# Attention probabilities left unnormalised, split in SBUF and transposed by DMA, with the outputs scaled in PSUM

## What is computed

```python
scores = jnp.einsum('bhqd,bhkd->bhqk', q, k) / scale
scores = jnp.where(causal[None, None], scores, -jnp.inf)
attn = jax.nn.softmax(scores, axis=-1)
out = jnp.einsum('bhqk,bhkd->bhqd', attn, v)
out = out.transpose(0, 2, 1, 3).reshape(B, S, N_HEADS * HEAD_DIM)
return out @ Wo
```

## Time and profile before

| | us |
|---|---|
| median of 3 runs | 739.17 (738.39 to 739.94) |
| the profiled execution | 737.62 |
| span of its instructions | 735.7 |
| attention loop rounds (from round 4 on), each | 31.52 |
| rounds 0 to 3 | 37.31, 39.92, 39.91, 34.10 |
| last round and epilogue | 35.1 |
| from there to the end | 163.5 |

### The profile page before, as it was taken

One profiled execution on the slowest core, in us unless ns is written; L12 is line 12 of the kernel. 1 busy time (PEld: TensorE's weight loads), 2 busy tenths in 40 slices (PEclk: granted clock), 3 DMA queues, 4 the chain that ended last, 5 costly groups with the idle time before them and its releaser, 6 DMA issues.

```text
span 735.7 us, 17233 instructions
## 1 busy us (share of the span) xinstructions
PE 659.1 (90%) x4994; PEld 460.8 (63%) x4995; DVE 581.6 (79%) x1683; ACT 442.3 (60%) x1205; POOL 537.8 (73%) x588
## 2 busy tenths in 40 slices
PE   3678869789999999999999999999987899999992
PEld 1255546556766667676666766667665577767761
DVE  6988879789999999998999999999876344333378
ACT  3585636465657666575675657668584664555542
POOL 4677777978888887888877888888988993555510
PEclk9899989999999999999999999999998999999996
DMA  9491000500000000000000000000122564665772
GB/s 306 165 301 48 1 0 2 141 22 16 0 14 14 0 14 0 14 7 7 14 0 14 0 14 14 0 14 2 35 70 88 167 117 105 138 141 138 210 285 101
DMA packets 64952, 50.44 MB, mean 69 GB/s; under 512 B 35252, under 2 KB 58260, under 8 KB 64916
## 3 DMA queue, kind: packets, MB, share of 16 engines
q1 hardware_dynamic: 60804, 39.45, 19.3%
q0 software_dynamic: 3840, 10.52, 4.3%
q10 hardware_dynamic: 272, 0.02, 0.0%
HBM read 24.72 MB, written 18.96 MB: 59 GB/s over the span
## 4 chain that ended last, share of the span: by engine, by line
POOL 41%; issue 19%; PE 17%; DVE 13%; ACT 7%; DMA 2%; POOLq 0%; SPq 0%; DVEq 0%
POOL arena L539 16%; PE bank L1546 8%; POOL arena L533 8%; POOL arena L526 7%; PE bank L1576 6%; POOL xs_dram L586 4%; ACT arena L777 3%; POOL compare L582 2%; PE bank L1555 2%; DVE arena L1108 2%; POOL arena L563 1%; ACT arena L785 1%; DVE arena L1082 1%; DVE arena L1083 1%; DVE arena L1078 1%
## 5 line engine op out<-in xcount | busy, mean ns | idle before, releaser
L539 POOL TENSOR_TENSOR arena<-arena,rinv 128x128 f32<-128x128 f32 (+3 forms) x256 | 176.4, 720 | 83.5 <-DVE rinv L1102 83.4
L777 ACT ACTIVATE arena<-bank,nmax 128x512 f32<-128x512 f32 (+3 forms) x256 | 132.5, 535 | 64.6 <-DVE nmax L1096 64.6
L1096 DVE CUSTOM_DVE_ANT_0 bank<-bank,mask_b 128x512 f32<-128x512 f32 (+3 forms) x256 | 118.1, 516 | 14.2 <-issue 14.2
L1390 PE MATMUL bank<-arena 128*128 128x512 f16 (+7 forms) x768 | 116.4, 302 | 5.9 <-POOL arena L533 5.9
L785 ACT CAST arena<-bank 128x512 f16<-128x512 f32 (+1 forms) x192 | 93.3, 522 | 45.1 <-PE bank L1403 43.5
L1359 PE MATMUL bank<-xnT_hi,arena 128*128 (+1 forms) x320 | 111.0, 389 | 9.2 <-DVE arena L1083 4.7
L1419 PE MATMUL bank<-arena 128*128 128x512 f16 (+7 forms) x768 | 118.0, 305 | 0.0
L1403 PE MATMUL bank<-ident_f,arena 128*128 128x128 f32 x640 | 93.5, 277 | 25.5 <-DVE arena L1108 14.5
L1108 DVE TENSOR_TENSOR arena<-bank,arena 128x512 bf16<-128x512 f32 (+1 forms) x192 | 109.0, 595 | 3.9 <-ACT arena L785 1.8
L526 POOL TENSOR_TENSOR arena<-arena 128x512 f32<-128x512 f32 x77 | 98.6, 1281 | 2.5 <-DVE arena L1083 2.2
L1403 PEld LDWEIGHTS bank<-ident_f,arena 128*128 128x128 f32 x640 | 74.0, 142 | 38.9 <-DVE arena L1108 18.3
(11 more groups left out here) (147 smaller groups left out, 1158.9 us busy)
## 6 DMA issues: line engine op xcount, KB each, us to landing
xs_dram<-s_sb SPq DMA_DIRECT2D x4, 1548.0 KB, 14.4
stage<-w_gate_up SPq DMA_DIRECT2D x16, 352.0 KB
arena<-ys_dram SPq DMA_DIRECT2D x8, 512.0 KB, 6.5
stage<-w_down SPq DMA_DIRECT2D x16, 176.0 KB
stage<-wq SPq DMA_DIRECT2D x4, 512.0 KB, 8.0
stage<-wo SPq DMA_DIRECT2D x4, 512.0 KB, 6.5
stage<-x SPq DMA_DIRECT2D x1, 2048.0 KB, 10.6
out<-s_sb SPq DMA_DIRECT2D x8, 256.0 KB, 2.1
```

Source lines behind the costliest of these rows:

```text
L539: ins = pool.tensor_tensor(pr, pr, rinv[:, par, qt:qt + 1].to_broadcast([P, (qt + 1) * P]), ALU.mult)
L777: ins = act.activation(probs[par][:, P_AT[qt]:P_AT[qt] + n], score_bank[u][:, col:col + n], ACT.Exp, scale=-1.0, bias=nmax[:, par, qt:qt + ...
L1096: ins = dve.tensor_tensor_reduce(score_bank[u][:, col:col + n], score_bank[u][:, col:col + n], mask_b[:, S - n:S], -1.0, 3e38, ALU.add, AL ...
L1390: ins = pe.matmul(score_bank[u][:, col:col + n_k], qT[a][:, j * S + qt * P:j * S + (qt + 1) * P], kT[m][:, 0:n_k], start=(n == 0), stop=(n ...
```

## The change

The inverse row sums are no longer multiplied into the probabilities. ScalarE writes the exponentials in the order in which their transposes are read (`exp_part`; the 512-wide row is cut in a 384-wide and a 128-wide part, and a small addition joins their sums, semaphore `totalled`), and casts all 1280 columns to float16 in one instruction (`p_hi`, one buffer for all heads). GpSimd makes the bfloat16 remainder (`low_probs`, `p_lo`, two buffers). SyncE transposes both with DMA from SBUF into `pT`, two DMAs for each head. TensorE makes four float32 transposes of the broadcast inverse sums for each head (`spread_inverse`), ScalarE copies them to `inverse` in SBUF, and VectorE multiplies the PV result in PSUM with it (`scale_output`) ahead of `output_hi` and `output_lo`. The output has two banks. The stage ring gets four slots and an order of its own, the zero fill is cut into 12 transfers that stand between the transposes, and experts 0 to 4 are loaded at other places. The core of the diff:

```diff
-            def divide(h, par):
-                pool.wait_ge(inverted, h + 1)
-                for qt in range(QT):
-                    pr = probs[par][:, P_AT[qt]:P_AT[qt] + (qt + 1) * P]
-                    ins = pool.tensor_tensor(pr, pr, rinv[:, par, qt:qt + 1].to_broadcast([P, (qt + 1) * P]), ALU.mult)
-                ins.then_inc(normed, 1)
+            def low_probs(rd, j):
+                h, par = rd.head(j), j % 2
+                pool.wait_ge(probs_hi, h + 1)
+                if not isinstance(h, int) or h >= 2:
+                    pool.wait_ge(lo_in[par], rd.landed(j) - 16)
+                if isinstance(h, int) and h == 1:
+                    pool.wait_ge(w_lo, W_FIRST)
+                pool.tensor_tensor(p_lo[par], probs[par], p_hi, ALU.subtract).then_inc(probs_lo, 1)
...
+            def transpose_probs(rd, j):
+                h, par = rd.head(j), j % 2
+                sp.wait_ge(probs_hi, h + 1)
+                if not isinstance(h, int) or h >= 2:
+                    sp.wait_ge(pv, h - 1)
+                sp.dma_start_transpose(pT[par][0].rearrange("p (g t) -> p g t", t=P), p_hi).then_inc(hi_in[par], 16)
+                sp.wait_ge(probs_lo, h + 1)
+                sp.dma_start_transpose(pT[par][1].rearrange("p (g t) -> p g t", t=P), p_lo[par]).then_inc(lo_in[par], 16)
...
+            def round_(rd):
+                for j in range(GH - 1 if rd.last else GH):
+                    transpose_probs(rd, j + 1)
+                    if rd.first or rd.second:
...
+                        for c in range(2 * rd.head(j), min(2 * rd.head(j) + 2, FILLS)):
+                            sp.dma_start(xs_tiles[:, c * FILL_TILES:(c + 1) * FILL_TILES], fill).then_inc(fill_out, 16)
...
+                if units[-1] == 2:
+                    last = rsum[:, par, QT - 1:QT]
+                    act.wait_ge(exped, h * 3 + 3)
+                    act.activation(last, rsum[:, par, QT:QT + 1], ACT.Identity, bias=last).then_inc(totalled, 1)
+                    if not isinstance(h, int) or h >= 1:
+                        act.wait_ge(hi_in[1 - par], rd.landed(j - 1))
+                        act.wait_ge(probs_lo, h)
+                    act.copy(p_hi, probs[par]).then_inc(probs_hi, 1)
+
+            def spread_inverse(rd, j):
+                h = rd.head(j)
+                act.wait_ge(spread_ps, h + 1)
+                if not isinstance(h, int) or h >= 1:
+                    act.wait_ge(o_scaled, h)
...
+                act.copy(inverse, rinv_bank[:]).then_inc(spread, 1)
...
+                    exponentials(rd, j + 1)
+                    if j > 0 or not rd.first:
+                        spread_inverse(rd, j - 1)
                     if j == 0:
...
                         rotate_hi("q3", rd.i * 5 + 5)
                         if not rd.first:
                             output_hi(rd, -1)
                         value_hi(rd)
...
+            def scale_output(rd, j):
+                dve.wait_ge(spread, rd.head(j) + 1)
+                dve.wait_ge(pv, rd.head(j) + 1)
+                dve.tensor_tensor(o_bank[j % 2][:], o_bank[j % 2][:], inverse, ALU.mult).then_inc(o_scaled, 1)
...
-                        rope("q0", (h, par))
                         if not rd.first:
-                            probs_lo(rd.head(j), j, (0, 1))
-                        if not rd.first:
+                            scale_output(rd, -1)
                             output_lo(rd, -1)
                         value_lo(rd)
...
+                for n, (a, m) in enumerate(((0, 0), (1, 0), (0, 1))):
+                    pe.wait_ge((hi_in, lo_in)[m][par], rd.landed(j))
+                    for kt in (0, 1, 3, 2):
+                        ins = pe.matmul(o_bank[par][:, kt * P:S], v_s[a][:, kt * DH:(kt + 1) * DH],
+                                        pT[par][m][:, PT_AT[kt]:PT_AT[kt] + (QT - kt) * P], start=(kt == 0 and n == 0), stop=(kt == 2 and n == 2))
                 ins.then_inc(pv, 1)
+
+            def spread_inverse(rd, j):
+                h = rd.head(j)
+                pe.wait_ge(inverted, h + 1)
+                if not isinstance(h, int) or h >= 1:
+                    pe.wait_ge(spread, h)
+                for qt in range(QT):
+                    ins = pe.transpose(rinv_bank[:, qt * P:(qt + 1) * P], rinv[:, j % GH, qt:qt + 1].to_broadcast([P, P]), ident_f[:])
+                ins.then_inc(spread_ps, 1)
```

More of the change, by code:

```diff
@@ L114, in head, with landed @@
         return self.i * GH + j
+    def landed(self, j):
+        return self.i * 32 + (j // 2 + 1) * 16
     def tile(self):
@@ L253, in build @@
         row_u = sb("row_u", [P, R_TILES], U32)
-        NSTG, SCOLS = 6, 1024
-        stage = sb("stage", [P, NSTG * SCOLS], F32)
-        ERING = 5
+        ERING, SCOLS = 5, 1024
+        KEPT = 3 * WE
+        stage = sb("stage", [P, ERING * WE], F32)
+        halves = [stage[:, KEPT + n * (PCOLS // 2):KEPT + (n + 1) * (PCOLS // 2)] for n in range(3)]
+        p_hi, p_lo = halves[0].bitcast(F16), [half.bitcast(BF16) for half in halves[1:]]
+        inverse = stage[:, KEPT + 3 * PCOLS // 2:KEPT + 3 * PCOLS // 2 + S]
         shared_s = [sb("shared_hi", [P, SHARED_W], F16), sb("shared_lo", [P, SHARED_W], BF16)]
@@ L659, in round_ @@
                         rows_low(rd.tile())
-                    divide(rd.head(j + 1), (j + 1) % 2)
+                    low_probs(rd, j + 1)
                     if j == 2 and not rd.last:
@@ L691, in round_ @@
                         shared_lo(1)
-                    divide(rd.head(GH), 0)
+                    low_probs(rd, GH)
                     rotate_lo("q2", rd.rot("q2"))
-                    if rd.first:
-                        pool.wait_ge(fill_out, 16 * FILLS)
-                        pool.memset(fill[:, :, D + 1], 0.0).then_inc(zeroed, 1)
             round_(Round(0, "first"))
@@ L700, in _ @@
             round_(Round(2, "third"))
+            pool.wait_ge(fill_out, 16 * FILLS)
+            pool.memset(fill[:, :, D + 1], 0.0).then_inc(zeroed, 1)
             scatter_tile(0)
@@ L772, in exponentials @@
+            def exponentials(rd, j, units=(0, 1, 2)):
+                h, par = rd.head(j), j % 2
+                if 0 in units and (not isinstance(h, int) or h >= 2):
+                    act.wait_ge(probs_lo, h - 1)
                 for u in units:
-                    unit = SCORE_UNITS[u]
                     act.wait_ge(maxed, h * 3 + u + 1)
-                    for qt, col in unit:
-                        n = (qt + 1) * P
-                        ins = act.activation(probs[par][:, P_AT[qt]:P_AT[qt] + n], score_bank[u][:, col:col + n], ACT.Exp, scale=-1.0,
-                                             bias=nmax[:, par, qt:qt + 1], accum_out=rsum[:, par, qt:qt + 1])
+                    for qt, col in SCORE_UNITS[u]:
+                        ins = exp_part(par, u, qt, range(min(qt + 1, QT - 1)), col, qt)
+                        if qt == QT - 1:
+                            ins = exp_part(par, u, qt, [qt], col + qt * P, QT)
@@ L859, in round_ @@
                     else:
-                        probs_hi(rd.head(j), j, (0, 1))
-                        exponentials(h, par)
                         if rd.first:
@@ L899, in _ @@
             round_(Round(NG - 1, "last"))
+            spread_inverse(EPILOGUE, -1)
             output_hi(EPILOGUE, -1)
-            for e in range(4, AHEAD):
+            for e in range(3, AHEAD):
                 expert_hi_part(e)
@@ L1451, in round_ @@
                 for j in range(GH - 1):
-                    h = rd.head(j)
-                    score(h + 1, j + 1, queries[j + 1], None, True)
+                    score(rd.head(j + 1), j + 1, queries[j + 1], None, True)
+                    if j > 0 or not rd.first:
+                        spread_inverse(rd, j - 1)
                     if j == 0:
@@ L1483, in round_ @@
                     project_out(rd, 2)
-                transpose_probs(rd.head(3), 3, (0, 1), rd.first)
                 weigh_values(rd, 2)
@@ L1488, in round_ @@
                     project(rd, "q3")
-                transpose_probs(rd.head(3), 3, (2,), rd.first)
                 if rd.first:
```

213 lines of the change are left out of this document (106 added, 107 removed).

## The result

| | before | after |
|---|---|---|
| median | 739.56 us | 778.47 us |
| ratio, 95% interval | | 1.053 (1.0513 to 1.0547) |
| profiled execution, span | 737.62, 735.7 | 778.42, 776.6 |
| rounds 0 to 3 | 37.31, 42.79, 37.04, 34.10 | 41.37, 43.24, 38.93, 38.23 |
| loop rounds from round 4 on | 31.52 | 34.03 to 34.05 |

Slower by 5.3%, 6 us beyond the forecast of 772. One correction to the table ahead of the prediction: it gives rounds 1 and 2 as 39.92 and 39.91; the value projection of round 2 starts at 119.27, so they last 42.79 and 37.04. Their sum, which the forecast used, is the same.

What follows compares the result with a forecast made beforehand. Bound: TensorE's work and an equally long wait chain through VectorE, ScalarE and GpSimd. Rounds gain 1.4 + 0.95 - 0.28, about 2.1 us; 14 rounds give 29.4, plus 3 + 0 + 1 makes 33, so 772 us; range 722 to 806.

Steps and rivals of the forecast that it cites:

- rival chain: Loop round: waits through scores 4, VectorE, ScalarE and GpSimd's lo k last 31.52 us, as long as TensorE's work.
- TensorE's saving: Loop round: six fewer transposes per head spare TensorE 2.6 us, which end up in its stalls.
- First stretch: Scores 4 to row maxima 2 on VectorE: 15.1 us instead of 13.68, 1.4 later.
- term of 0.8 us for the landing: Cast of head 1 on ScalarE waits for the previous head's DMA transpose, starting at 10.6 instead of 9.8 us.
- rival 3: Stalls drop TensorE's clock, passing on 0.5 to 1.5 us; late landing adds 1.1; 35 us rounds, 795 us; chance 0.22.
- rival 2: DMA transposes land within 4 us; rounds of 32.8 us, 760 us in all, still slower than before; chance 0.16.
- DMA's price: SyncE's ten-block transposes: 2.35 us to issue, 4.7 us to landing, bounds 2.6 and 5.8.
- Small costs on ScalarE and GpSimd: Per head: ScalarE about 1.05 us more, its 1280-column cast 1.26; GpSimd's 1280-column subtraction 2.61, 0.14 less work.
- release of GpSimd: Row maxima 2 to GpSimd's start: 4.9 us instead of 3.95, 0.95 later.
- GpSimd's stretch: GpSimd's work from its release until scores 4 can start: 13.89 us before, 0.28 shorter after the change.
- wait ahead of scores 4: Sign in the profile: TensorE waits over 2 us for GpSimd's lo k ahead of scores 4.
- The ends: Outside the loop: 3 us for early fills, 0 for last round and epilogue, 1 for expert loads; rounds 1 and 2 get 2.1 each.

Runs made afterwards that it cites:

- padded kernel: Changed kernel with ten spread transposes per head where four are needed, 24 more a round; ratio 1.0408 to the kernel before.
- unread matmuls: Changed kernel with six 512-column matmuls that nobody reads queued on TensorE ahead of scores 4; ratio 1.0387, rounds of 32.93 us.
- best order: Changed kernel with head 3's low part behind lo k and the sum of q2, q2 earlier, plus other reorderings; ratio 0.9815, rounds of 29.19 us.
- one small transfer: Changed kernel with one awaited 8-byte transfer on SyncE ahead of each high transpose; ratio 1.0559, loop rounds 33.8 us on average.
- two small transfers: Changed kernel with two awaited 8-byte transfers on SyncE ahead of each high transpose; ratio 1.0763, loop rounds 34.8 us on average.

## Why the prediction was right, and where not

- **Direction and rival chain: right.** The bound is a chain by way of scores 4, row maxima and GpSimd's lo k, and TensorE's saving (2.6 us a round) does not shorten it. The padded kernel shows it, more sharply than I had put it: 24 transposes more, an estimated 2.6 us of TensorE's work (24 x 0.109), left the round where the unread matmuls had it. TensorE has 3.7 us of idle in a round; I had said some 5, with 28.4 busy. It is busy for 30.29, since slow matmuls count as busy: with the clock held it is 28.41 in the best order, as forecast.
- **First stretch, 15.1 forecast, 15.64 measured: two errors that nearly cancel, so that the time came out near by luck in this term.** I let the cast of head 1 wait until 10.6; without that wait the stretch was 9.8 + 4.5 = 14.3. Measured, the cast starts at 10.88 and row maxima 2 come 4.76 later. The cast is late because row maxima 1 start 7.47 us after scores 4 (6.24 before); 1.09 of that 1.23 is the slow scores 4 and q3, since it is 6.38 with unread matmuls. The term of 0.8 us for the landing measured 0, because the transfer was priced too high; its place was right, as the kernel with one small transfer shows, whose cast of head 1 waits 0.3 to 0.4 us in the rounds behind a scores 4 at full clock. The term for the clock, priced in rival 3, was left out of the sum. My own round without the landing's term was 32.8; with the clock held the chip gave 32.93. The right account of the round is rival 2 with rival 3: 32.9 + 1.1.
- **The DMA's price: wrong.** Ten blocks from SBUF are issued in 1.34 us where I took 2.35; landing is 3.4, not 4.7. The issue hardly grows with blocks (1.19 for four in the earlier trace rows). The rule that I set aside comes nearer: the Trainium skill, "Advanced Engine Details and Errata", section "X-Bar Transpose (TRN2)", has transposes as fast as regular DMAs. Regular transfers of 256 and 516 KB land in 2.1 and 4.9 us; on a line between them 328 KB take an estimated 2.9, and the transpose needs 3.4.
- **Small costs on ScalarE and GpSimd: right.** Cast 1.24 us (1.26 forecast), release of GpSimd 4.80 (4.9), low part 2.62 (2.61), scaling 0.69 (0.65), GpSimd's stretch 13.58 (13.61).
- **Rival 3** came true in its first half: the clock takes 1.1 us a round by the run with unread matmuls, inside the 0.5 to 1.5 that I let it pass on. The slow stretch costs TensorE 1.7 us (5.92 us from scores 4 to scores 1 for 4.24). Its second half, 1.1 us for a late landing, did not. The wait ahead of scores 4 was 2.03, as the prediction said ("over 2 us").
- **The ends were mis-sized.** Rounds 0 to 3 with what lies ahead grew by 12.3 us where the forecast has 3 + 3 x 2.1 = 9.3. In round 0 VectorE waits 9.1 us for ScalarE's high parts of the input (3.3 before); in round 3 it waits 3.2 us for GpSimd's memset of the fill, a wait that I did not price. The granted clock of rounds 0 to 3 is 0.83, 0.88, 0.91 and 0.96, before 1.00, 0.92, 1.00 and 1.00. Round 14 was -0.5 (forecast +2.1), the one in which the clock did not fall, the end +3.9 (forecast +1; ScalarE waits 5.3 us for experts' weights there, before 2.9). How much the clock and each of these waits are worth in the end was not measured apart.

```profile
DVE xnT_lo L1065 <- ACT xnT_hi L793: 9.1, 3, 5.1
```

```profile
DVE waited L1159 <- POOL s_sb L749: 3.2, 1, 3.2
```

(the first from the waits of round 0, the second from those of round 3.)

- **What the prediction did not see:** that the change frees an order. By taking the transposes off TensorE it lets head 3's piece of GpSimd's work stand behind lo k, which is worth 3.2 us a round after the change and costs 6.0 before it.

## What to carry to other kernels

Work taken off the busiest engine is worth nothing while a chain of waits is as long as its work; it can even cost, if TensorE's clock falls behind the longer wait, and then a few unread matmuls in the wait are a quick test of how much. Look at the granted clock of each round before taking an average: rounds of one run differed by it, and an average over both kinds hid half of what two small transfers cost at full clock. When a change removes a consumer from an engine's hand-written order, look again at what its producer may now do later: here one moved instruction (3.2 us) was worth more than the 2.6 us of TensorE's work that was saved. And test the terms of a round that came out right one by one, since two wrong terms (here 0.8 us for a landing that cost nothing, and 1.1 us of the clock left out) can hide each other.

## What the runs showed of the hardware

- A DMA transpose of 128 x 1280 two-byte elements from SBUF to SBUF is issued in 1.34 us and lands in 3.4; 128 x 512 from DRAM took 1.19 and 3.3 (median). An 8-byte transfer with its wait costs SyncE's queue 1.33 us (1.12 in the kernel with one: 370.65 to 371.77).
- Behind a wait of 2.03 us TensorE ran some 3.3 us at the 1.2 GHz level, starts 0.43 us apart for 0.22; behind waits of 0.75 and 1.38 us it kept 2.4 GHz in all of rounds 4 to 13. Behind 3.45 us nearly all of scores 4 were slow (3.02 us for 1.64).
- The same wait did not always do it: TensorE kept 2.4 GHz behind 2.04 us in five of ten rounds (one small transfer), behind 2.37 us in round 14 of the changed kernel, behind 3.42 us in the kernel with reciprocals and copy moved (round 4), and behind 3.42 us in the kernel before with its division moved (round 5).
- A multiplication of 512 columns in PSUM by a factor in SBUF, written back to PSUM, takes VectorE 0.69 us, as much as a low part that ends in SBUF.
